# A selective scan's step in a new order on TensorE and VectorE, with a convolution tile's taps placed one by one

## The reference

```
res = h;  u = layernorm(h)
z, xBC, dt = split(u @ in_w.T)            # 512, 640, 8 columns
dt  = softplus(dt + dt_bias)
xBC = silu(depthwise_conv(xBC, 4 taps) + conv_b)
x, B, C = split(xBC)                      # 8 heads x 64, 64, 64
state = exp(dt*A)*state + (dt*x) outer B  # token by token
y = state . C + D*x
y = rmsnorm(y * silu(z)) * rms_w
h = y @ out_w.T + res
```

## Time and profile before

| | us |
|---|---|
| median of 3 runs | 2253.24 (2248.58 to 2256.14) |
| the profiled execution, its own time | 2254.19 |
| its span | 2252.4 |
| TensorE busy | 1964.3 (87%) |
| VectorE busy | 1571.0 (70%) |
| ScalarE busy | 1265.0 (56%) |
| GpSimd busy | 933.5 (41%) |

### The profile page before, as it was taken

How to read it: one execution, slowest core, us unless ns; L and a number is a source line. 1 busy time by engine, 2 the same in 40 slices (tenths; PEclk the granted TensorE clock), 3 DMA queues, 4 the chain that set the end, 5 groups by cost and what they waited for, 6 DMA issues and landing times. The chain is left out here.

```text
span 2252.4 us, 37459 instructions
## 1 busy us (share of the span) xinstructions
PE 1964.3 (87%) x12544; PEld 1396.2 (62%) x12544; DVE 1571.0 (70%) x3503; ACT 1265.0 (56%) x2237; POOL 933.5 (41%) x840
## 2 busy tenths in 40 slices
PE   5899999999999989889999999899984888888887
PEld 4566656666666666556666666566653667677675
DVE  4667777677677757676766677766635788888886
ACT  3666666656665656666556666665531454444443
POOL 2555566555555534544444445544440111111111
PEclk8999998999999979999999999999985999999999
DMA  3011111111111101111111111110003011111100
GB/s 129 15 34 34 43 51 33 37 33 33 33 33 37 53 9 43 52 34 38 33 33 33 33 33 52 41 33 28 24 14 104 24 57 56 56 56 56 56 19 19
DMA packets 87251, 91.68 MB, mean 41 GB/s; under 512 B 4929, under 2 KB 82449, under 8 KB 87185
## 3 DMA queue, kind: packets, MB, share of 16 engines
q1 hardware_dynamic: 79360, 79.46, 10.8%
q10 hardware_dynamic: 7824, 11.37, 2.0%
HBM read 57.26 MB, written 25.17 MB: 37 GB/s over the span
## 5 line engine op out<-in xcount | busy, mean ns | idle before, releaser
L374 PE MATMUL L_front<-L_uhi,L_whi 128*128 128x512 f32 x576 | 268.4, 466 | 114.7 <-DVE L_xc L1055 111.0
L840 POOL TENSOR_TENSOR L_yg<-L_yg,L_sz 128x512 f32<-128x512 f32 x128 | 163.8, 1280 | 278.2 <-DVE L_yg L1082 278.2
L1567 POOL TENSOR_TENSOR M_rstd<-M_var,M_power 128x4 f32<-128x4 f32 x64 | 69.8, 1091 | 464.0 <-DVE M_var L156 464.0
L374 PEld LDWEIGHTS L_front<-L_uhi,L_whi 128*128 128x128 f32 x576 | 113.7, 197 | 227.3 <-DVE L_xc L1055 162.8
L848 POOL TENSOR_TENSOR L_xc<-L_xpad,L_vec 128x512 f32<-128x512 f32 x160 | 165.9, 1039 | 204.4 <-ACT L_xpad L655 204.4
L1067 DVE TENSOR_TENSOR L_m<-L_dbank,L_gm 128x512 f32<-128x512 f32 x256 | 175.0, 684 | 100.2 <-ACT L_dbank L695 100.2
L374 PE MATMUL L_front<-L_uhi,L_wlo 128*128 128x512 f32 x576 | 241.5, 419 | 0.0
L374 PE MATMUL L_front<-L_ulo,L_whi 128*128 128x512 f32 x576 | 240.4, 417 | 0.0
L524 PE MATMUL L_mix<-L_wo,L_yg 128*128 128x256 f32 x1024 | 234.1, 382 | 0.8 <-POOL L_yg L840 0.8
L1525 ACT ACTIVATE M_nrm<-M_lin,M_shift,M_rstd 128x256 f32<-128x256 f32 x192 | 92.8, 564 | 243.2 <-POOL M_shift L1575 243.2
L689 ACT ACTIVATE L_sz<-L_front,L_pbias 128x512 f32<-128x512 f32 x128 | 87.9, 687 | 246.4 <-PE L_front L374 246.4
(11 more groups left out here) (175 smaller groups left out, 4787.0 us busy)
## 6 DMA issues: line engine op xcount, KB each, us to landing
h<-L_hres SPq DMA_DIRECT2D x32, 512.0 KB, 3.0
L_hin<-in_x SPq DMA_DIRECT2D x16, 512.0 KB, 4.6
L_hres<-in_x SPq DMA_DIRECT2D x16, 512.0 KB, 3.9
L_cc<-L_xc ACTq DMA_DIRECT2D x64, 128.0 KB, 2.3
L_hin<-h SPq DMA_DIRECT2D x16, 512.0 KB, 4.7
L_hres<-h SPq DMA_DIRECT2D x16, 512.0 KB, 3.9
M_hin<-h SPq DMA_DIRECT2D x16, 512.0 KB, 3.8
M_xin<-in_x SPq DMA_DIRECT2D x16, 512.0 KB, 4.6
```

The source lines that it names most:

```text
L374: last = nc.tensor.matmul(to[:, :], ww[:, kd, tile * P:(tile + 1) * P], a[:, kd, :], start=i == 0, stop=i == len(passes) - 1)
L840: nc.gpsimd.tensor_tensor(yg[:, t, :], yg[:, t, :], sz[:, t, :], ALU.mult).then_inc(y_gated, 1)
```

## The change

Three things are done.

First, TensorE's list for a step is in a new order. The second half of `result` of the item before moves ahead of decay 4 and transpose 0, `turn_dt` behind them; `outputs` 0 moves ahead of conv tile 4, the first `new_state` ahead of outputs 1; the four z projections, which stood between outputs and states, follow each other behind outputs 3; the decays 0 and 1 of the next item stand ahead of the second `new_state` and the scores.

Second, VectorE's list is in a new order to go with it. `convolve` takes a further argument, `step`, and each of the three taps is a call of its own, so other work can stand between them. `layer_moments` moves to the head of the step, `bias_dt` behind `finish` and the first `scale_x`. `add_state` is split in two calls, and the first waits for all four outputs. At a layer's start `mean_square` and `finish` come before `fold_weights`.

Third, helpers are split so that this can be written (`rest_u` by half, `decay_operands` and `first_operands`, `within` and `carried` outside of `outputs`).

The core of the diff:

```diff
@@ TensorE, step
                 if more:
                     project_conv(n + 1, 0)
-                    turn_dt(n + 1)
+                if follows_any(n):
+                    result(n - 1, layer_of(n, layer, -1), 1)
                 decays(n, 4)
                 turn_x(n, p, 0)
-                if follows_any(n):
-                    result(n - 1, layer_of(n, layer, -1), 1)
+                if more:
+                    turn_dt(n + 1)
+                turn_x(n, p, 1)
                 decays(n, 5)
                 if more:
                     project_conv(n + 1, 1)
-                turn_x(n, p, 1)
                 turn_x(n, p, 2)
+                turn_x(n, p, 3)
                 decays(n, 6)
                 if more:
                     project_conv(n + 1, 2)
-                turn_x(n, p, 3)
+                decays(n, 7)
                 turn_b(n, p)
-                decays(n, 7)
...
                 carry(n, 2)
                 carry(n, 3)
+                outputs(n, p, 0)
                 if more:
                     project_conv(n + 1, 4)
-                outputs(n, p, 0)
+                new_state(n, 0)
                 outputs(n, p, 1)
                 if more:
                     sum_da(n + 1)
                 outputs(n, p, 2)
-                if more:
+                outputs(n, p, 3)
+                if more:
+                    turn_cum(n + 1)
                     project_z(n + 1, 0)
-                    turn_cum(n + 1)
-                outputs(n, p, 3)
-                if more:
                     project_z(n + 1, 1)
-                new_state(n, 0)
-                if more:
                     project_z(n + 1, 2)
+                    project_z(n + 1, 3)
+                    decays(n + 1, 0)
+                    decays(n + 1, 1)
                 new_state(n, 1)
                 if more:
-                    project_z(n + 1, 3)
-                    start_scan(n + 1, 1 - p)
+                    scores(n + 1, 1 - p)
@@ VectorE, convolve
-            def convolve(n, layer, p, i):
+            def convolve(n, layer, p, i, step):
...
+                if step == 0:
+                    dve.wait_ge(tap0, QCONV * n + i + 1)
+                    nc.vector.scalar_tensor_tensor(acc, acc, weight(3), to, ALU.mult, ALU.add).then_inc(taps, 1)
+                elif step == 1:
+                    dve.wait_ge(taps, 3 * QCONV * n + 3 * i + 1)
...
@@ VectorE, add_state
-            def add_state(n, p):
-                dve.wait_ge(sdec_done, n + 1)
+            def add_state(n, p, s):
+                if s == 0:
+                    dve.wait_ge(sdec_done, n + 1)
+                    dve.wait_ge(y_ready, T * n + T)
+                dve.wait_ge(st_ready, 2 * n + s + 1)
@@ VectorE, step
                     set_halo(n + 1, 1 - p)
-                    bias_dt(n + 1, layer1)
-                weigh(n, 3)
                 if more2:
                     layer_moments(n + 2, layer2, chunk2, p)
-                scale_x(n, p, 0)
-                weigh(n, 4)
+                weigh(n, 3)
+                if more:
+                    convolve(n + 1, layer1, 1 - p, 0, 0)
+                    convolve(n + 1, layer1, 1 - p, 0, 1)
                 if follows_any(n):
                     finish(n - 1, layer_of(n, layer, -1), None, 1 - p, 1)
...
                 if more:
                     mask_scores(n + 1)
                     weigh(n + 1, 0)
+                if starts_layer(n + 2):
+                    fold_rows(layer2)
                 if more2:
-                    if starts_layer(n + 2):
-                        fold_rows(layer2)
-                    rest_u(n + 2)
-                    if starts_layer(n + 2):
-                        fold_weights(layer2)
+                    rest_u(n + 2, 0)
+                    rest_u(n + 2, 1)
+                if more:
+                    weigh(n + 1, 1)
                 mean_square(n)
                 if more:
-                    weigh(n + 1, 1)
+                    weigh(n + 1, 2)
                 finish(n, layer, c, p, 0)
-                if more:
-                    weigh(n + 1, 2)
                 if starts_layer(n + 2):
+                    fold_weights(layer2)
                     keep_bias(layer2)
```

More of the change, by code:

```diff
@@ L474, in new_state, with within, carried @@
                 last.then_inc(st_ready, 1)
+            def within(n, t, b):
+                for odd in range(2):
+                    half = slice(HD * odd, HD * odd + HD)
+                    nc.tensor.matmul(ybank[t % 2][half, b * P:(b + 1) * P], dtx[:, b, 2 * t + odd, :], m[:, b, 2 * t + odd, :],
+                                     start=b == 0, stop=False, skip_group_check=True)
+            def carried(n, p, t, b):
+                for odd in range(2):
+                    half = slice(HD * odd, HD * odd + HD)
+                    made = nc.tensor.matmul(ybank[t % 2][half, b * P:(b + 1) * P], state[p][half, b, t, :], cs[half, b, t, :],
+                                            start=False, stop=True, skip_group_check=True)
+                return made
             def outputs(n, p, t):
@@ L482, in outputs @@
                 wait(pe, y_skip, T * n + t - 1)
[L483 to L496, removed]
                 if t == 0:
@@ L968, in round_constants, with rest_u @@
                 nc.vector.tensor_copy(sel[:, :, :], staged[:, NH * P:NH * P + 2 * P].rearrange("p (o m) -> p o m", o=2)).then_inc(consts_ready, 1)
[L970 to L973, removed]
+            def rest_u(n, kd):
+                dve.wait_ge(u_hi, KD * n + kd + 1)
+                nc.vector.tensor_tensor(ulo[:, kd, :], front[kd][:, :], uhi[:, kd, :].bitcast(F32), ALU.subtract).then_inc(u_lo, 1)
             def bias_dt(n, layer):
@@ L1021, in decay_operands, with first_operands @@
                                             ALU.mult, ALU.add).then_inc(dops, 1)
+            def first_operands(n):
                 dve.wait_ge(dops, 2 * n + 2)
@@ L1049, in weight @@
                     return vector(layer, "conv_w", q * TAPS + tap, 1)
[L1051 to L1055, removed]
+                if step == 0:
[3 more added lines that the diff above has]
+                    dve.wait_ge(taps, 3 * QCONV * n + 3 * i + 1)
+                    nc.vector.scalar_tensor_tensor(acc, xpad[:, q, :, 1:1 + P], weight(1), acc, ALU.mult, ALU.add).then_inc(taps, 1)
+                else:
+                    dve.wait_ge(taps, 3 * QCONV * n + 3 * i + 2)
+                    nc.vector.scalar_tensor_tensor(to, xpad[:, q, :, 2:2 + P], weight(2), acc, ALU.mult, ALU.add).then_inc(taps, 1)
             def mask_scores(n):
@@ L1114, in front_part @@
                 fold_weights(0)
-                rest_u(n)
+                for kd in range(KD):
+                    rest_u(n, kd)
                 round_constants()
@@ L1121, in front_part @@
                 finish_dt(n, 0, p)
-                convolve(n, 0, p, 0)
+                for tap in range(TAPS - 1):
+                    convolve(n, 0, p, 0, tap)
                 for i in range(1, QCONV):
-                    convolve(n, 0, p, i)
+                    for tap in range(TAPS - 1):
+                        convolve(n, 0, p, i, tap)
                     if i == 3:
@@ L1128, in front_part @@
                         decay_operands(n)
+                        first_operands(n)
                 start_scan(n)
-                rest_u(n + 1)
+                for kd in range(KD):
+                    rest_u(n + 1, kd)
                 weigh(n, 1)
@@ L1145, in step @@
                     set_halo(n + 1, 1 - p)
-                    bias_dt(n + 1, layer1)
-                weigh(n, 3)
                 if more2:
                     layer_moments(n + 2, layer2, chunk2, p)
-                scale_x(n, p, 0)
-                weigh(n, 4)
+                weigh(n, 3)
+                if more:
+                    convolve(n + 1, layer1, 1 - p, 0, 0)
+                    convolve(n + 1, layer1, 1 - p, 0, 1)
                 if follows_any(n):
                     finish(n - 1, layer_of(n, layer, -1), None, 1 - p, 1)
+                scale_x(n, p, 0)
                 if more:
-                    convolve(n + 1, layer1, 1 - p, 0)
+                    bias_dt(n + 1, layer1)
+                    convolve(n + 1, layer1, 1 - p, 0, 2)
                 scale_x(n, p, 1)
-                weigh(n, 5)
+                weigh(n, 4)
                 scale_x(n, p, 2)
                 scale_x(n, p, 3)
+                weigh(n, 5)
+                if more:
+                    convolve(n + 1, layer1, 1 - p, 1, 0)
+                    convolve(n + 1, layer1, 1 - p, 1, 1)
                 weigh(n, 6)
                 if more:
-                    convolve(n + 1, layer1, 1 - p, 1)
-                weigh(n, 7)
+                    convolve(n + 1, layer1, 1 - p, 1, 2)
+                    convolve(n + 1, layer1, 1 - p, 2, 0)
                 scale_c(n, 0)
                 scale_c(n, 1)
+                weigh(n, 7)
                 if more:
```

(2 more changed lines are left out.)

36 lines of the change are left out of this document (19 added, 17 removed).

## The result

| | before | after |
|---|---|---|
| median of 4 runs, us | 2254.69 | 2123.61 (2120.03 to 2125.94) |
| ratio, 95% interval | 1 | 0.942 (0.9396 to 0.9445) |
| profiled execution, its own time | 2254.19 | 2123.9 |
| mean granted clock | 0.937 | 0.963 |

The kernel became 5.8% faster. 2142 was forecast, with 2098 to 2200 as the range.

The account below looks back on a forecast made before the run. TensorE's own work plus waits for VectorE, and clock falls, bound the scan. Step 50.44 to 47.0 us gains 107 over 31 steps, with the layer change 111: 2254.2 to 2143, median 2142; range 2098 to 2200.

Parts of the forecast that it names:

- What bounds: Scan: TensorE's own work plus its waits for VectorE; holes before tiles 3 and 4 also make the clock fall.
- Point 1, the head: Step start: GpSimd's tap holds a small moments instruction, 1.0 us dearer; transpose 1 newly waits 0.7 us for `finish`.
- Rival A: Step start: the moments' small instructions don't block; step 46.1 us, time 2114 us; chance 0.16.
- Point 2, tile 3: Tile 1 to tile 3: wait before tile 3 0.85 us in place of 2.03, plus 0.3 for ScalarE's copy of B.
- Point 3, tile 4: Tile 4, now behind outputs 0: no wait in place of 1.64 us; up to 1 us if `scale_c` slips.
- Point 4, the sums: Sums after outputs 1: a 0.4 us wait in layer 0, none in layer 1; the two 0.3 us waits go.
- Point 5, the end: Step end: later `add_state`, skips and gates leave `result` 2.5 us of cover; the last step stays unchanged.
- rival B: Stretch before tile 3: the clock still falls; 2199 us if in every step, 2170 in half; chance 0.18.
- Rival C: GpSimd's queue ahead of tile 1's tap slips into the wait before tile 3; 2272 us at 4.2 us slip; chance 0.06.
- The layer change: Layer change: `mean_square` passes ahead of `fold_weights`, saving 4.5 of the bias matmuls' 5.16 us wait.
- The sum: Whole kernel: step 44.96 + 2.05 = 47.0 us, scan gain 107 us, 111 with the layer change, time 2142 us.
- the 44.96 us stand: Scan step: TensorE's own work at full clock stays 44.96 us, since no instruction's work is added or removed.

Follow-up runs that it names:

- moments_split: Changed kernel with the moments' small instructions behind tile 0's first tap and tile 0's second tap moved behind `bias_dt`: 2093.66 us, ratio 0.929.
- before_filled_one: Kernel before with seven matmuls that nobody reads ahead of conv tile 3, none ahead of tile 4: 2242.78 us, ratio 0.9983.
- fold_first: Changed kernel with `fold_weights` ahead of `mean_square` and `finish` again at the layer change: 2131.37 us, ratio 0.9459.
- z0_early: Changed kernel with the first z projection ahead of `turn_cum` and outputs 3 again: 2130.92 us, ratio 0.9483.
- tile1_taps_together: Changed kernel with `weigh` 6 behind tile 1's last tap, so that tile's three taps stand together: 2123.59 us, ratio 0.943.
- both: moments_split with `weigh` 6 behind tile 1's last tap as well: 2094.59 us, ratio 0.9315.
- fine_waits: moments_split with outputs 0 waiting for the two weighs of each piece instead of all eight at its start: 2088.08 us, ratio 0.9286.
- tile4_first: Changed kernel with conv tile 4 ahead of outputs 0 again on TensorE: 2233.66 us, ratio 0.991.
- before_outputs_first: Kernel before with outputs 0 ahead of conv tile 4 on TensorE and nothing else: 2214.92 us, ratio 0.9858.

## Why the prediction was right, point by point

*What bounds.* The holes on TensorE and the clock behind them did bound the scan. Filling the old holes with useless work recovered 34 of the 37 us that the mean step (50.44 against 49.26, 31 times) assigns to the clock.

*Point 1, the head.* The block was taken at 1.0 us from the earlier trace rows; the instruction took 1.02 in the step shown, 0.87 more than alone. So an instruction of 4 elements is held like `finish_dt` in the earlier trace rows. The wait before transpose 1 was 0.87 to 0.94 us in most steps of layer 0 and 0.74 to 0.78 in layer 1, against 0.7. Rival A, by which the small instructions don't block, falls. Its price of 0.9 a step stays untested, since moments_split changed two things.

*Point 2, tile 3.* 0.65 us against 0.85. The 0.3 for ScalarE's copy of B came too, as 0.42 in the carries.

*Point 3, tile 4.* No wait, as laid out, but 0.27 us before outputs 0 for `weigh` 7, which I had missed.

*Point 4, the sums.* The wait of 0.4 us in layer 0 didn't come outside the first two steps: outputs 1 ends as tile 3's last tap does. The two waits of 0.3 went.

*Point 5, the end.* The later `add_state`, skips and gates cost nothing in the loops. The last step was forecast as unchanged and was not: `result` waits 4.10 us there for the gate, 0.82 before, and then takes 5.41 us at a granted clock of 0.68, in place of 3.69 at 1.00.

*The clock.* 1.00 in the whole step, so rival B didn't come: here 0.65 us after transposes and carries did not bring the clock down. The argument used against B was wrong all the same: it took both old holes to be needed, and before_filled_one shows falls with one of 1.64 us. No row shows that transposes count less. Rival C's chain runs through GpSimd as told (tile 1's first tap still waits 0.28 us for it), but didn't slip.

*The layer change.* 4.5 us forecast, 4.4 shown by fold_first.

*The sum.* The step was forecast at 47.0 us; without the layer change's interval the mean is (1446.7 - 56.71)/30 = 46.33. That is the whole miss: 31 x 0.67 = 21 us against 18.4 between 2142 and 2123.6. The waits are not in it. With the 0.42 in the carries they come to about 2.0 to 2.3 us in the steps of the loops, against 2.05. That is partly luck: transpose 1 (0.93 against 0.7), the copy of B (0.42 against 0.3) and outputs 0 (0.27, not foreseen) were dearer, tile 3 and the sums (0.4 in layer 0, didn't come) cheaper.

The term that was mis-sized is "the 44.96 us stand". TensorE's own work fell to 46.52 - 2.27 = 44.25, 0.7 less. One z projection and the start of what follows it, before (matmuls of the projection left out):

```profile
557.57 0.50 PE L374 MATMUL L_front<-L_uhi,L_whi 128*128 128x512 f32 x1
...
559.15 1.08 PE L472 MATMUL L_mix<-L_wx,L_bt 128*64 128x256 f32 x8
```

and after, the first matmuls of the second, third and fourth projection of a row:

```profile
475.09 0.39 PE L374 MATMUL L_front<-L_uhi,L_whi 128*128 128x512 f32 x1
...
476.48 0.40 PE L374 MATMUL L_front<-L_uhi,L_whi 128*128 128x512 f32 x1
...
477.88 0.40 PE L374 MATMUL L_front<-L_uhi,L_whi 128*128 128x512 f32 x1
```

A projection that `new_state` follows takes 1.58 us. In the row the second and the third take 1.39 and 1.40, and the last, with decay 0 behind it, 1.49. In the steps of the earlier trace rows and of the timeline after, all four and `turn_cum` take 6.69 and 5.84 us without waits: that is 0.85 less, and other new neighbours cost part of it again. One run bears on it: in z0_early one projection leaves the row, and the same matmuls take 6.08 us in place of 5.86 in a step of layer 1. Why neighbours of one kind follow each other faster is not shown.

## What to carry to other kernels

Lay a reordered step out by hand from the old trace's durations: it gave each wait to within 0.4 us, with errors that cancelled, and the sum's error was in what I had called constant, TensorE's work, which depends on what follows what. Price a hole on TensorE at its length and at the clock that may fall behind it: here 66 and 44 us for the same hole, and a few matmuls that nobody reads, put in the hole, separate the two. Before moving a short VectorE instruction with two SBUF operands, look at what GpSimd runs at its new place. And where taking away one wait leaves the step as it was, as in tile1_taps_together and both, another engine's list may be the chain: look for what stands in it ahead of the instruction that is waited for, as moments_split did. Read both layers: a wait can come back in one and not in the other, as in fine_waits. And change one thing at a time: moments_split changed two, and their prices can't be told apart.

## What the runs showed of the hardware that was not expected

- A VectorE instruction of 0.15 us on 4 elements takes up to 1.03 us beside a GpSimd one and ends with it. The statistics, which read one SBUF tensor each, take 1.40 us for four beside such a tap and 1.40 without one.
- Long holes before single tiles brought the granted clock from 1.00 to 0.50 in part of the steps: one of 2.50 us (tile4_first, with 0.93 and 0.65 before it), one of 2.03 (before_outputs_first) and one of 1.64 (before_filled_one). Those of 0.93 and 0.65 us alone did not. After the fall in tile4_first the engine was busy without a pause for 6 us at 0.50.
- Twelve useless matmuls of 512 columns a step made the kernel before 34 us faster.
